# A gated recurrence beside a mixture of experts on one core: the recurrent products stream 2 columns in place of 20 or 40

## The chip, the cores and the metric

The kernel runs on one NeuronCore of a Trainium2 chip. The metric is device time in microseconds (us) of one execution. An execution with the profiler on was recorded as well; its instruction times are the source of every number below that is not a median.

## The reference, cut to what matters

The input `x` has shape (2, 1024, 256). A mixture of four experts plus a shared branch is added to it, and then a gated recurrence over the 1024 positions is added to that. The recurrence is serial in time:

```python
def step(h, xs):
    xzt, xrt, xht = xs
    z = jax.nn.sigmoid(xzt + h @ U_z + vz)
    r = jax.nn.sigmoid(xrt + h @ U_r + vr)
    hh = jnp.tanh(xht + r * h @ U + vh)
    h_new = (1.0 - z) * h + z * hh
    return (h_new, h_new)
...
x = x + _L0_cond_ref(x, cond_1024, ...)
x = x + _L1_cond_ref(cond_1024, x, ...)
```

The batch of `x` is B = 2, so the state has 2 rows of 256 numbers. With features on the 128 partitions, one recurrent product of one 128x128 weight tile has 2 columns of data.

## The kernel before, in words

The sequence is cut into 8 chunks of 128 positions, a chunk into 8 bodies of 16 steps: 64 bodies, 1024 steps. A chunk's hidden layer of 1024 is cut into 8 slices, so chunk c+1's feed-forward is 8 tiles, and one tile is done beside each body of chunk c. Chunk 0's feed-forward and the first tile of chunk 1 come before the recurrence starts.

All order on TensorE is written by hand. `gru_body` (L953) does a step as follows. It waits for the first half of the state (`h_parts`, HI), does the products of the reset gate R with it, three tiles of the update gate Z, then R's products with the low half of the state (LO), and the rest of Z. Then comes `gap_work` window 0. It waits for `p_parts` (reset gate times state, HI and LO, written by VectorE at L716 and L719), does the products of the candidate C, and then `gap_work` window 1. ScalarE takes the tanh of each gate (L507), VectorE makes the new state with scans at L730 and L732.

A recurrent product is made by `recur` (L911, its matmul is L918). Each gate has 4 weight tiles of 128x128; the weights are split in two fp16 parts, `u_high` and `u_mid`. HI is multiplied by both parts, LO by `u_high` alone, so a gate has 12 matmuls and a step 36. R and Z stream `H_FILL` = 20 columns, C streams `FILL` = 40. Only the first 2 carry data; the others are zeros, set once by VectorE in `p_parts` and `h_parts`, and are added to later columns of the same PSUM bank, to which they add nothing.

`gap_work` (L926) fills the time in which TensorE waits for the other engines. With a feed-forward tile it does units of it (`up` at L856, `down` at L874); a unit is half of one fp32 product of 256 columns, and the profile shows it as two matmuls of 128 columns. A tile has 40 units. The table `FFN_UNITS` gives window 0 one unit, window 1 one unit or, at t = 4 to 10, 12 and 14, two; at t = 15 the second window has none left. At t = 1 `turn_body` transposes the finished body. In the last body of a chunk, where a next chunk follows, `gate_input` (L888) is put into 12 windows, two matmuls of 256 columns each, and `output_bias` (L829) into t = 3. The last 8 bodies have neither; there `gap_work` issues idle matmuls on a constant tile (L950), one of 256 columns in window 0, two of 512 in window 1. Body 55 has `gate_input` but no feed-forward, and no idle matmuls.

`inject` (L903) starts a body by writing the input part of each gate into its PSUM bank, three matmuls of 64 columns a gate.

Of the kernel before, what the change touches and what calls it, by code (L numbers as in the profile page):

```python
# [27 lines left out]
F16 = mybir.dt.float16  # L28
# [3 lines left out]
P = 128  # L32
# [7 lines left out]

FILL = 40
H_FILL = 20
IDLE_FILL = (256, 512)


def moe_gru_kernel(nc, x, cond, gate_w, gate_b, time_w, time_b, ew1, eb1, ew2, eb2, sw1, sb1, sw2, sb2,
                   w_z, u_z, c_z, b_z, w_r, u_r, c_r, b_r, w_h, u_h, c_h, b_h, branch_mask, out):
    B, T, D = x.shape  # L50
    E, _, H = ew1.shape
    BR = E + 1
    KC = D // P
# [6 lines left out]
    SC = STEPS * B  # L60
    ST = KC * B
# [41 lines left out]
    with ctx:  # L103
        def sb(name, shape, dt=F32):
            return ctx.enter_context(nc.sbuf_tensor(name, shape, dt))

        def pb(name):
            return ctx.enter_context(nc.psum_tensor(name, [P, 512], F32))
# [56 lines left out]
        spread = sb("spread", [B, BR, B])  # L165


        p_parts = sb("p_parts", [P, 2, KC, FILL], F16)
        keep_warm = sb("keep_warm", [P, max(IDLE_FILL)], BF16)
        h_parts = sb("h_parts", [P, 2, FILL // B, 2 * ST], F16)  # L170
        HI, LO = range(2)
        blend = sb("blend", [P, 2 * ST])
        half_h = sb("half_h", [P, ST])
# [3 lines left out]
        gate_ps = [pb("r_ps"), pb("z_ps"), pb("c_ps")]  # L177
# [585 lines left out]
        def _(pe):  # L763
            mm = pe.matmul
# [5 lines left out]
            for i in range(CH):  # L770
# [7 lines left out]
                for k in range(KC):  # L778
                    for b in range(B):
                        at = (k * B + b) * P  # L780
                        last = pe.transpose(xp_ps[i % 2][:, at:at + P], x_rows[:, i, b, k * P:(k + 1) * P],
                                            ident[:, :])
# [27 lines left out]
            for g in range(GATES):  # L810
                for m in range(KC):
                    at = (g * KC + m) * B
                    for k in range(KC):
                        last = mm(gate_ps[0][:, at:at + B], cf[:, g, k, m * P:(m + 1) * P], cond_v[:, k, :],
                                  start=(g == 0 and m == 0 and k == 0), stop=(k == KC - 1),
                                  skip_group_check=True)
# [94 lines left out]
            def recur(g, t, part, i, weights, tile, stop=False):  # L911

                m, k = tile
                width = FILL if part is p_parts else H_FILL
                moving = (p_parts[:, i, k, :] if part is p_parts else
                          h_parts[:, i, 0:H_FILL // B, (2 * k) * B + 1:(2 * k + 2) * B:2])
                for at, w in enumerate(weights):
                    last = mm(gate_ps[g][:, m * SC + t * B:m * SC + t * B + width],  # L918
                              w[:, g, k, m * P:(m + 1) * P], moving, start=False,
                              stop=stop and k == KC - 1 and at == len(weights) - 1,  # L920
                              skip_group_check=True)
                return last
# [30 lines left out]
            def gru_body(n, ffn, tail, last):  # L953
                cols = chunk_columns(ffn[0]) if ffn else None
                tail_cols = chunk_columns(tail) if tail is not None else None
                for t in range(STEPS):
# [4 lines left out]
                    for tile in TILES:  # L961
                        recur(R, t, h_parts, HI, BOTH, tile)
# [3 lines left out]
                    for tile in TILES[:early]:  # L966
                        recur(Z, t, h_parts, HI, BOTH, tile)
                    pe.wait_ge(part_ready, before_n + 4)
                    for tile in TILES:
                        last_mm = recur(R, t, h_parts, LO, HIGH, tile, stop=True)  # L970
# [82 lines left out]
```

## Time and profile before

| | |
|---|---|
| median of 3 runs | 2317.78 us (2313.11 to 2319.58) |
| the profiled execution, its own time | 2310.71 us |
| its span | 2308.9 us |
| mean granted TensorE clock | 0.975 |
| TensorE busy (matmul) | 2157.9 us, 93% |
| VectorE, ScalarE, GpSimdE busy | 1200.4, 679.3, 344.0 us |

PE is TensorE's matmuls, PEld its weight loads, DVE VectorE, ACT ScalarE, POOL GpSimdE. A granted clock of 1.00 is TensorE's level of 2.4 GHz, 0.50 is that of 1.2 GHz. Matmuls overlap in the array: the time from one start to the next is what a product costs in a stream, the duration is how long one is in flight. A line with x4 merges four instructions that follow each other, from the first start to the last end.

### The profile page before, as it was taken

What the parts mean: (1) busy time and instruction counts of PE and PEld (TensorE: products, weight loads), DVE (VectorE), ACT (ScalarE), POOL (GpSimd) and SP (SyncE); (2) the same over time, 40 slices, a digit from 0 to 9 for tenths busy, and PEclk for the clock granted to TensorE, in tenths of its full rate; (3) what the DMA queues carried; (4) which work ended last, traced back from release to release, by engine and by line L of the source; (5) the groups of instructions that cost most, each with busy time, mean ns of one, the idle gap of its engine ahead of it and who ended that gap; (6) DMA issues with size and microseconds to landing.
All of it is one profiled execution on the core that took longest, in us unless ns stands there. A gap on an engine that the chain in (4) does not pass through costs nothing.

```text
span 2308.9 us, 108165 instructions
## 1 busy us (share of the span) xinstructions
PE 2157.9 (93%) x42955; PEld 1785.3 (77%) x43019; DVE 1200.4 (52%) x10473; ACT 679.3 (29%) x3670; POOL 344.0 (15%) x684
## 2 busy tenths in 40 slices
PE   7999999999999999999999999999999999988888
PEld 6787888887887888888888788888788888755555
DVE  5245555555545555555545555555554555555554
ACT  2332233232232232322233222323223223222222
POOL 3011111111111111111102111111111111110000
PEclk8999999999999999999999999999999999899999
DMA  5411111111111111111111111111111111000000
GB/s 159 125 55 45 44 41 40 44 41 43 45 38 45 43 42 41 45 40 45 41 40 45 40 47 39 40 45 40 45 43 40 40 45 42 11 4 4 4 4 4
DMA packets 143478, 97.21 MB, mean 42 GB/s; under 512 B 13664, under 2 KB 142999, under 8 KB 143004
## 3 DMA queue, kind: packets, MB, share of 16 engines
q1 hardware_dynamic: 141840, 90.49, 13.5%
q8 instruction: 338, 5.54, 1.0%
q14 instruction: 136, 1.11, 0.2%
q10 hardware_dynamic: 1164, 0.07, 0.0%
HBM read 88.41 MB, written 2.10 MB: 39 GB/s over the span
## 4 chain that ended last, share of the span: by engine, by line
PE 88%; DVE 5%; issue 4%; ACT 4%; POOL 0%; POOLq 0%; ACTq 0%; DVEq 0%
PE c_ps L918 22%; PE r_ps L918 19%; PE y_ps L874 15%; PE up_ps L856 13%; PE z_ps L918 12%; DVE h_parts L730 3%; ACT c_ps L507 2%; PE up_ps L950 2%; PE xp_ps L888 2%; DVE p_parts L716 1%; ACT r_ps L507 1%; PE xp_ps L898 1%; PE y_ps L829 0%; DVE hidden L278 0%; PE z_ps L903 0%
## 5 line engine op out<-in xcount | busy, mean ns | idle before, releaser
L918 PE MATMUL r_ps<-h_parts,u_high 128*128 128x20 f16 x8192 | 609.6, 180 | 82.3 <-DVE h_parts L730 49.9
L918 PEld LDWEIGHTS r_ps<-h_parts,u_high 128*128 128x128 f16 x8192 | 429.9, 96 | 260.3 <-DVE h_parts L730 149.5
L918 PEld LDWEIGHTS c_ps<-p_parts,u_high 128*128 128x128 f16 x8192 | 415.4, 96 | 203.1 <-DVE p_parts L716 139.1
L918 PE MATMUL c_ps<-p_parts,u_high 128*128 128x40 f16 x8192 | 530.8, 183 | 42.2 <-DVE p_parts L716 24.3
L918 PE MATMUL z_ps<-h_parts,u_high 128*128 128x20 f16 x8192 | 568.0, 179 | 0.0
L856 PE MATMUL up_ps<-feat,up_w 128*128 128x128 f32 (+1 forms) x2380 | 528.0, 315 | 0.0
L874 PE MATMUL y_ps<-hidden,down_w 128*128 128x128 f32 (+1 forms) x2380 | 507.9, 319 | 6.1 <-DVE hidden L278 6.1
L716 DVE SCALAR_TENSOR_TENSOR p_parts<-r_ps,h_hist 128x4 f16<-128x4 f32 x1024 | 165.9, 162 | 606.0 <-ACT r_ps L507 606.0
L918 PE MATMUL z_ps<-h_parts,u_mid 128*128 128x20 f16 x4096 | 439.6, 179 | 0.0
L918 PEld LDWEIGHTS z_ps<-h_parts,u_high 128*128 128x128 f16 x8192 | 427.8, 96 | 0.0
L507 ACT ACTIVATE r_ps<-r_ps 128x4 f32<-128x4 f32 x1024 | 161.8, 158 | 821.8 <-PE r_ps L918 821.8
L730 DVE TENSOR_TENSOR_SCAN h_parts<-c_ps,blend 128x8 f16<-128x8 f32 x1024 | 177.5, 173 | 387.7 <-ACT c_ps L507 387.7
L507 ACT ACTIVATE c_ps<-c_ps 128x4 f32<-128x4 f32 x1024 | 161.8, 158 | 711.9 <-PE c_ps L918 711.9
L874 PEld LDWEIGHTS y_ps<-hidden,down_w 128*128 128x128 f32 x2380 | 354.0, 197 | 16.3 <-issue 12.7
L856 PEld LDWEIGHTS up_ps<-feat,up_w 128*128 128x128 f32 x2380 | 358.2, 191 | 8.7 <-issue 3.0
L918 PE MATMUL c_ps<-p_parts,u_mid 128*128 128x40 f16 x4096 | 340.2, 180 | 0.0
L918 PE MATMUL r_ps<-h_parts,u_mid 128*128 128x20 f16 x4096 | 337.7, 179 | 0.0
L918 PEld LDWEIGHTS z_ps<-h_parts,u_mid 128*128 128x128 f16 x4096 | 299.0, 96 | 0.0
L918 PEld LDWEIGHTS c_ps<-p_parts,u_mid 128*128 128x128 f16 x4096 | 259.2, 97 | 4.9 <-issue 0.6
L918 PEld LDWEIGHTS r_ps<-h_parts,u_mid 128*128 128x128 f16 x4096 | 257.0, 97 | 6.9 <-issue 2.2
L722 DVE TENSOR_SCALAR blend<-z_ps,half_s 128x4 f32<-128x4 f32 x1024 | 218.6, 214 | 0.0
L719 DVE TENSOR_TENSOR p_parts<-r_ps,p_parts 128x4 f16<-128x4 f32 x1024 | 166.6, 163 | 35.6
(132 smaller groups left out, 2139.0 us busy)
## 6 DMA issues: line engine op xcount, KB each, us to landing
up_w<-in_L_cond_ew SPq DMA_DIRECT2D x256, 128.0 KB, 2.4
down_w<-in_L_cond_ew SPq DMA_DIRECT2D x256, 128.0 KB, 2.1
up_w<-in_L_cond_sw SPq DMA_DIRECT2D x64, 128.0 KB, 2.4
down_w<-in_L_cond_sw SPq DMA_DIRECT2D x64, 128.0 KB, 2.1
x_rows<-in_x SPq DMA_DIRECT2D x8, 256.0 KB, 5.0
out<-out_rows SPq DMA_DIRECT2D x128, 16.0 KB, 1.8
cf<-in_L_cond_C_r SPq DMA_DIRECT2D x1, 256.0 KB, 5.7
cf<-in_L_cond_C_z SPq DMA_DIRECT2D x1, 256.0 KB, 5.8
```

The costliest lines, as they stand in the source:

```text
L507: act.activation((c_now, tanh_r, tanh_z)[(g + 1) % GATES].rearrange("p (m b) -> p m b", b=B), gate_v[g][:, :, t, :], ACT.Tanh, scale=0.5 / ...
L716: dve.scalar_tensor_tensor(p(HI), tr, 1.0, prev, ALU.add, ALU.mult).then_inc(part_ready, 1)
L719: dve.tensor_tensor(p(LO), sq(product), p(HI), ALU.subtract).then_inc(part_ready, 1)
L722: dve.tensor_scalar(blend_v[:, :, 0], tz, 1.0, half_s[:, :], ALU.add, ALU.mult).then_inc(state, 1)
L730: dve.tensor_tensor_scan(h_parts[:, HI, 0, :], cand, blend[:, :], 0.0, ALU.mult, ALU.add).then_inc(part_ready, 1)
L856: last = mm(up_ps[e % 2][:, at:at + width], up_w[:, e, k, :], cols[k, half], start=(k == 0 and at == 0), stop=(k == KC - 1), skip_group_ch ...
L874: last = mm(y_ps[:, m * COLS + at:m * COLS + at + width], down_w[:, e, m * P:(m + 1) * P], hidden[:, e % 2, at:at + width], start=False, s ...
L888: last = mm(xp_ps[g % 2][:, m * COLS:(m + 1) * COLS], wx[:, g, k, m * P:(m + 1) * P], cols[k, None], start=(m == 0 and k == 0), stop=(k == ...
L898: last = pe.transpose(rows_ps[0:SC, k * P:(k + 1) * P], out_feat[:, k, :], ident[:, :])
L918: last = mm(gate_ps[g][:, m * SC + t * B:m * SC + t * B + width], w[:, g, k, m * P:(m + 1) * P], moving, start=False, stop=stop and k == K ...
L950: mm(up_ps[0][:, 0:IDLE_FILL[window]], ident16[:, :], keep_warm[:, 0:IDLE_FILL[window]], start=True, stop=True, skip_group_check=True)
```

## The change

Every recurrent product streams B = 2 columns. The two constants go, and the tiles shrink to the columns that carry data. The number and order of instructions, all waits, the idle matmuls and the feed-forward units stay.

```diff
-FILL = 40
-H_FILL = 20
 IDLE_FILL = (256, 512)
...
-        p_parts = sb("p_parts", [P, 2, KC, FILL], F16)
+        p_parts = sb("p_parts", [P, 2, KC, B], F16)
         keep_warm = sb("keep_warm", [P, max(IDLE_FILL)], BF16)
-        h_parts = sb("h_parts", [P, 2, FILL // B, 2 * ST], F16)
+        h_parts = sb("h_parts", [P, 2, 1, 2 * ST], F16)
...
             def recur(g, t, part, i, weights, tile, stop=False):

                 m, k = tile
-                width = FILL if part is p_parts else H_FILL
                 moving = (p_parts[:, i, k, :] if part is p_parts else
-                          h_parts[:, i, 0:H_FILL // B, (2 * k) * B + 1:(2 * k + 2) * B:2])
+                          h_parts[:, i, 0, (2 * k) * B + 1:(2 * k + 2) * B:2])
                 for at, w in enumerate(weights):
-                    last = mm(gate_ps[g][:, m * SC + t * B:m * SC + t * B + width],
+                    last = mm(gate_ps[g][:, m * SC + t * B:m * SC + t * B + B],
                               w[:, g, k, m * P:(m + 1) * P], moving, start=False,
                               stop=stop and k == KC - 1 and at == len(weights) - 1,
                               skip_group_check=True)
```

## Rows read from the trace of the kernel before

**Rows 1.** The page: busy time of TensorE, and its granted clock in 40 slices.
```profile
PE 2157.9 (93%) x42955; PEld 1785.3 (77%) x43019; DVE 1200.4 (52%) x10473; ACT 679.3 (29%) x3670; POOL 344.0 (15%) x684
...
PEclk8999999999999999999999999999999999899999
```

**Rows 2.** The page: shares of the chain that ended last, by engine.
```profile
PE 88%; DVE 5%; issue 4%; ACT 4%; POOL 0%; POOLq 0%; ACTq 0%; DVEq 0%
```

**Rows 3.** Groups by line and form; busy us, mean ns of one, then idle time before.
```profile
L918 PE MATMUL c_ps<-p_parts,u_high 128*128 128x40 f16 x8192 | 530.8, 183 | 42.2 <-DVE p_parts L716 24.3
```

**Rows 4.** Timeline of a one-unit step at full clock: start us, us, instruction.
```profile
1032.35 0.18 PE L918 MATMUL r_ps<-h_parts,u_high 128*128 128x20 f16 x1
...
1032.72 0.25 PE L918 MATMUL r_ps<-h_parts,u_high 128*128 128x20 f16 x4
...
1033.01 0.16 ACT L507 ACTIVATE r_ps<-r_ps 128x4 f32<-128x4 f32 x1 [0.92 <-PE r_ps L918]
...
1033.42 0.19 PE L918 MATMUL c_ps<-p_parts,u_high 128*128 128x40 f16 x1
...
1033.69 0.27 PE L918 MATMUL c_ps<-p_parts,u_high 128*128 128x40 f16 x4
...
1033.99 0.16 ACT L507 ACTIVATE c_ps<-c_ps 128x4 f32<-128x4 f32 x1 [0.68 <-PE c_ps L918]
1034.42 0.18 PE L918 MATMUL r_ps<-h_parts,u_high 128*128 128x20 f16 x1
```

**Rows 5.** Busy time by stretch, all engines; after POOL the granted clock, DMA share, GB/s.
```profile
123.00:2043.00 1920.00, 1819.25 (x37572) 1547.30 (x37572) 1012.22 (x9064) 579.41 (x3164) 305.81 (x616) 0.97 0.14 41
...
401.00:404.40 3.40, 3.02 (x71) 2.49 (x70) 1.73 (x17) 1.08 (x5) 0.61 (x1) 1.00 0.12 36
404.50:407.90 3.40, 3.40 (x54) 3.32 (x51) 1.67 (x15) 1.15 (x6) 0.73 (x1) 0.50 0.02 5
...
2029.30:2032.60 3.30, 2.11 (x59) 1.67 (x54) 1.72 (x15) 1.06 (x7) 0.00 (x0) 1.00 0.01 2
2032.70:2042.80 10.10, 8.17 (x170) 6.24 (x172) 5.01 (x46) 2.49 (x15) 4.58 (x11) 0.50 0.01 2
```

**Rows 6.** The same view, PE records of L856 (`up`) alone, with the clock.
```profile
401.10:404.50 3.40, 1.37 (x6) 1.00 0.10 30
...
414.70:418.10 3.40, 0.78 (x5) 1.00 0.13 38
```

**Rows 7.** The same stretches, PE records of L874 (`down`) alone.
```profile
401.10:404.50 3.40, 0.06 (x1) 1.00 0.10 30
...
414.70:418.10 3.40, 1.16 (x6) 1.00 0.13 38
```

**Rows 8.** Timeline of a two-unit step at half clock: start us, us, instruction.
```profile
1911.24 0.23 PE L918 MATMUL r_ps<-h_parts,u_high 128*128 128x20 f16 x1
...
1911.66 0.26 PE L918 MATMUL r_ps<-h_parts,u_high 128*128 128x20 f16 x4
...
1911.93 0.77 PE L874 MATMUL y_ps<-hidden,down_w 128*128 128x128 f32 x2
1911.96 0.16 ACT L507 ACTIVATE r_ps<-r_ps 128x4 f32<-128x4 f32 x1 [0.96 <-PE r_ps L918]
...
1912.50 0.24 PE L918 MATMUL c_ps<-p_parts,u_high 128*128 128x40 f16 x1
...
1912.80 0.30 PE L918 MATMUL c_ps<-p_parts,u_high 128*128 128x40 f16 x4
1912.94 1.20 PE L856 MATMUL up_ps<-feat,up_w 128*128 128x128 f32 x4
...
1913.93 0.23 PE L918 MATMUL r_ps<-h_parts,u_high 128*128 128x20 f16 x1
```

**Rows 9.** Timeline at half clock: two idle matmuls of window 1.
```profile
2041.64 1.06 PE L950 MATMUL up_ps<-keep_warm,ident 128*128 128x512 bf16 x2
```

**Rows 10.** Timeline of ScalarE: the first tanh of the recurrence.
```profile
123.85 0.16 ACT L507 ACTIVATE r_ps<-r_ps 128x4 f32<-128x4 f32 x1 [1.80 <-PE r_ps L918]
```

## The prediction

> **What bounds the kernel now.** I read the page first. TensorE is busy 93% of the span and its granted clock is nearly full in every slice [rows 1]; the chain of waits gives it 88% of the path [rows 2]. A share says little here, because TensorE runs filler and feed-forward work in its gaps, so I went to the timeline. The recurrence starts at about 123 us [rows 10], and all 1024 steps come after it. In the step of [rows 4] TensorE is not the limit. R's first product starts at 1032.35 and the next step's at 1034.42, 2.07 us later. Between them lies one serial chain: R's products, tanh at 1033.01, VectorE, C's first product at 1033.42, C's products, tanh at 1033.99, the scan, and the next R at 1034.42. From the tanh of R to C's first product is 0.41 us, from the tanh of C to the next R 0.43 us. The feed-forward lies beside this chain as long as it fits into those gaps. The widths to be cut: 40 columns for C, 183 ns a product in flight [rows 3], 20 for R [rows 4] and alike for Z.
>
> **The change, part by part, at full clock.** The instruction count stays, so the price of a product is its spacing and the latency of the last one. Spacing: the x4 line of R lasts 0.25 us, one of them 0.18, so three spacings are 0.07 and one is 25 ns (rounded) [rows 4]. The x4 line of C cannot be used for this, because its wait for the low half widens it. But 12 products of C at 40 columns, 17 ns of streaming at 2.4 GHz, cannot be below those 25 ns, and 20 columns are 8 ns. [...] Saving: nothing. Latency: R's last product starts at 1032.72 + 0.07 = 1032.79, its tanh at 1033.01, 0.22 later. C's last starts at 1033.69 + 0.09 = 1033.78, its tanh at 1033.99, 0.21 later [rows 4]. Twenty columns and forty have the same delay, although 20 columns are 8 ns of streaming. So at full clock I take zero for the whole edit. Bounds: a loss has no source in fewer columns at an equal clock; a gain is at most the streaming itself, 18 columns of R and 38 of C, 7.5 + 16 = 23.5 ns, 24 us over 1024 steps. The shorter memsets lie before 123 us behind the feed-forward and the waits for matrices, and are nothing.
>
> [...]
>
> **The change, the clock.** This is the step I weigh most. The clock is at half in some pieces of the recurrence, 0.97 on average from 123 to 2043 us [rows 5]. What did TensorE do before it fell? From 2029.3 to 2032.6, still at full clock, it had only recurrent products (59 records, no idle matmul, no feed-forward); from 2032.7 on it was at half [rows 5]. From 401.1 to 404.5 it had the light steps at the start of a body, 6 + 1 feed-forward records [rows 6, 7], and fell at 404.5 [rows 5]; from 414.7 to 418.1, in heavier steps, it had 5 + 6 such records and stayed at full [rows 6, 7]. It was not idle before the fall at 404.5, but busy 3.02 of 3.40 us [rows 5]. It fell where the least arithmetic was streamed, and recurrent products alone, filler and all, did not hold it.
>
> Now count a step in column passes. A feed-forward record at 1.2 GHz has 213 ns: four records fill 1912.94 to 1913.93 [rows 8], 0.99 us less 0.14 of turn-over (what two records take there above 2 x 213, 1911.93 to 1912.50), which is 256 cycles for 128 columns, two passes. A light step (two units, four records) has 4 x 256 = 1024 passes and 24 x 20 + 12 x 40 = 960 of the recurrence, 1984 in all, and after such steps the clock has fallen. After the change the heaviest ordinary step (three units) has 1536 + 36 x 2 = 1608, the light one 1096. So every ordinary step will stream less than those after which the clock fell. The zeros seem to do nothing but carry the clock. I forecast the half clock through nearly the whole recurrence.
>
> **Price of a step at half clock, 2 columns.** From [rows 8]: R and Z take 1911.24 to 1911.93, 0.69 us; the x4 line is 0.26, a spacing of 27 ns, so 20 columns (17 ns at 1.2 GHz) are hidden here too, and 0.69 stays. One unit: 1911.93 to 1912.50, 0.57. C's block: 1912.50 to 1912.94, 0.44, at (0.30 - 0.20)/3 = 33 ns a product, which is 40 columns at 1.2 GHz; at 2 columns it goes down to the 27 of R, 11 x 6.7 = 0.07 less, 0.37. Two units: 0.99. A two-unit step is 0.69 + 0.57 + 0.37 + 0.99 = 2.62 us and TensorE has no gap in it. In a one-unit step the second half is 0.37 + 0.57 = 0.94 by TensorE, but by the chain 0.34 to the start of C's last product, 0.21 to its tanh and 0.43 to the next R, 0.98; the step is 1.26 + 0.98 = 2.24. (R's tanh at 1911.96 comes 0.22 after the last R product, as at full clock.)
>
> **The sum.** A body has 7 one-unit steps (t = 15 counted so) and 9 two-unit steps: 15.7 + 23.6 = 39.3 us, plus some 0.6 for six injections of 64 columns at 53 ns and the transposes, an estimate: 39.9. Of 55 bodies with feed-forward, 49 are ordinary: 1955. Six end a chunk and add 24 `gate_input` records of 256 columns, 427 ns each, and four of `output_bias`: 12 us, 51.9 each; these stream most, the clock may come back inside them, so I take 50: 300. Body 55 has no feed-forward: 16 x 2.1 and about 6 for `gate_input`: 40. In the last 8 bodies a step is 0.72 (R to its tanh [rows 8]) + 0.41 + C's 0.34 + the two idle matmuls of 512 columns, 427 ns each at 1.2 GHz (1.06 together with the latency of the last [rows 9]), 0.85, 2.33 us; 16 steps and 0.4 are 37.7, times 8 is 302. With 123 before and 5 behind: 123 + 1955 + 300 + 40 + 302 + 5 = 2725 us. That is against the profiled execution, span 2308.9 and time 2310.71, 2 us apart; the median of the runs is 7 above it. I predict 2730. What late work is next? VectorE, ScalarE and the transfers keep their times, so with slower TensorE they only wait longer; nothing new comes onto the path.
>
> **Rivals.** (A) Half clock nearly throughout: 2730. (B) It alternates: in the heavier steps the clock comes back. For: pieces at half end by themselves, and those steps keep their feed-forward. Against: they stream less per time than the steps at half clock in [rows 8], which carried 960 passes more. If seven of nine two-unit steps return to 2.07, 49 x 7 x 0.55 = 189 us go, and 37 in the last 8 bodies with them at full clock (33.1 a body): about 2510. (C) The clock cares for work in flight, not for columns: TensorE keeps issuing a product every 25 ns, nothing changes, 2318, or a few us more with more pieces at half. Against it is the fall at 404.5 us, with TensorE busy before it [rows 5]. [...] (D) The other side: the clock holds and latency falls with the columns. Its place is the last product of R and of C, its price the 23.5 ns a step, its condition that the delay of 0.21 to 0.22 is not a floor: 2294. (That the change doesn't do what it says is excluded: both branches of `moving` and the output go to 2 columns.)
>
> **How the numbers follow.** A 0.75, B 0.13, C 0.07, D 0.05. The bound for no change is 0.3%, 7 us, about what this measurement can tell. C falls half or so inside it: same 0.06, faster 0.05, slower 0.89. A alone holds 2640 (clock back in the last 8 bodies and in the chunk ends) to 2770 (transitions and waits that the sum leaves out). To leave out no more than 2 in 10 the range goes on to B's middle: 2530 to 2770.
>
> **What would show it.** In the changed profile the PEclk line should stand at 5 from about the fourth slice to the end; the mean clock about 0.55. C's spacing at half clock should be 27 ns, not 33; a two-unit step 2.62 us, a one-unit step 2.24; the delay to the tanh 0.22 for all gates. TensorE's idle time before C should vanish in feed-forward steps. I am wrong if the line keeps 9 over most slices (C or D), or shows 7 to 8 (B); if steps at half clock cost other than 2.24 and 2.62, the sum is.

## The result, and the profile after

| | before | after |
|---|---|---|
| median of 3 runs | 2317.78 us | 2679.53 us (2667.41 to 2679.92) |
| profiled execution, time and span | 2310.71, 2308.9 us | 2679.92, 2678.1 us |
| mean granted clock | 0.975 | 0.537 |
| matmul records in the trace | 42955 (64 missing; weight loads 43019) | 43019 |

The change makes the kernel slower, by a ratio of 1.156 (95% interval 1.1504 to 1.1616). The forecast was 2730, within 2530 to 2770. The work is the same; TensorE does nearly all of the recurrence at a granted clock of 0.50.

The page of the changed kernel, the lines that answer to [rows 1, 2], and two groups by line (answering to [rows 3]; the recurrent matmuls are on L915 now, the tanh on L505, the feed-forward on L854 and L872, the idle matmuls on L947):

```profile
PE 2626.8 (98%) x43019; PEld 2351.0 (88%) x43019; DVE 1198.8 (45%) x10473; ACT 686.9 (26%) x3670; POOL 344.9 (13%) x684
...
PEclk8955556555565555555565555655556555555555
...
PE 95%; DVE 2%; ACT 2%; issue 1%; DMA 0%; SPq 0%; POOL 0%; POOLq 0%; ACTq 0%; DVEq 0%
...
L915 PE MATMUL r_ps<-h_parts,u_high 128*128 128x2 f16 x8192 | 618.9, 169 | 20.5 <-DVE h_parts L728 19.6
...
L915 PE MATMUL c_ps<-p_parts,u_high 128*128 128x2 f16 x8192 | 519.7, 170 | 9.4 <-DVE p_parts L714 2.6
```

The clock line stands at 5 from the third slice on, with a 6 in five slices. TensorE's share rises from 93% to 98% and its share of the chain from 88% to 95%. Its idle time before C's products falls from 42.2 to 9.4 us. In the nine two-unit steps of a body it is the bound throughout: R's first product starts 0.63 us after the start of the scan that makes the state (L728), where it was 0.23. In most one-unit steps (t = 0, 2, 11, 15) that stays 0.23 us, so there the second half of the step still goes by the chain. VectorE's busy time is that of before to 2 us. A product is in flight for less time than before, 170 ns against 183, and yet everything takes longer. The busy times by stretch, in the columns of [rows 5]:

```profile
130.00:415.00 285.00, 283.08 (x4775) 267.24 (x4775) 128.75 (x1155) 72.10 (x393) 38.05 (x75) 0.50 0.12 35
417.00:433.00 16.00, 15.81 (x293) 13.93 (x291) 7.23 (x65) 6.50 (x31) 1.34 (x2) 1.00 0.18 51
434.00:744.00 310.00, 307.79 (x5140) 289.40 (x5138) 138.67 (x1244) 78.89 (x428) 42.60 (x86) 0.50 0.13 36
...
2360.00:2670.00 310.00, 300.58 (x5206) 187.87 (x5204) 147.84 (x1328) 65.93 (x408) 22.28 (x56) 0.50 0.01 3
```

The clock falls as soon as the recurrence begins, at 126.5 us. It comes back for 14 to 17 us in each of the six bodies that have feed-forward and `gate_input` together, and falls again. From 2048 us on it never comes back, in body 55 (`gate_input` without feed-forward) as little as in the last 8. TensorE is busy 99% of the first of these stretches: the clock is low with the engine supplied. Now single steps, to set beside [rows 8, 9]:

```profile
1011.14 0.24 PE L915 MATMUL r_ps<-h_parts,u_high 128*128 128x2 f16 x4
...
1011.40 0.77 PE L872 MATMUL y_ps<-hidden,down_w 128*128 128x128 f32 x2
1011.42 0.16 ACT L505 ACTIVATE r_ps<-r_ps 128x4 f32<-128x4 f32 x1 [1.01 <-PE r_ps L915]
...
1012.23 0.24 PE L915 MATMUL c_ps<-p_parts,u_high 128*128 128x2 f16 x4
1012.34 1.20 PE L872 MATMUL y_ps<-hidden,down_w 128*128 128x128 f32 x4
1012.51 0.16 ACT L505 ACTIVATE c_ps<-c_ps 128x4 f32<-128x4 f32 x1 [0.78 <-PE c_ps L915]
...
1013.75 0.24 PE L915 MATMUL r_ps<-h_parts,u_high 128*128 128x2 f16 x4
...
2500.40 0.21 PE L915 MATMUL r_ps<-h_parts,u_high 128*128 128x2 f16 x1
...
2502.72 0.21 PE L915 MATMUL r_ps<-h_parts,u_high 128*128 128x2 f16 x1
```

A two-unit step lasts 13.75 - 11.14 = 2.61 us, a step of the last bodies 2.32. C's x4 line is 0.24 where it was 0.30 at this clock. And from the last product (1011.14 + 0.08) to the tanh at 1011.42 there are 0.20 us, for C (1012.23 + 0.08 to 1012.51) as well: less than the 0.21 to 0.22 of [rows 4].

The prediction's 2.4 and 1.2 GHz stand for columns a ns. In the kernel before, two idle matmuls of 512 columns in a row last 0.59 us at a clock of 1.00 and one alone 0.38 (2103.95 and 2102.10 us), so they start 0.21 us apart: 2.4 columns a ns. At 0.50 the two last 1.06 [rows 9], each 0.63, and start 0.43 us apart: 1.2 columns a ns.

### The profile page after: what moved, and what is told of

It is laid out like the page before. It is cut to its first block, busy times and chain, and to the rows that moved or that the text cites. A ratio compares the mean times of both kernels' runs of the same rounds, so it can differ in the third digit from the quotient of the medians.

```text
span 2678.1 us, 108229 instructions
## 1 busy us (share of the span) xinstructions
PE 2626.8 (98%) x43019; PEld 2351.0 (88%) x43019; DVE 1198.8 (45%) x10473; ACT 686.9 (26%) x3670; POOL 344.9 (13%) x684
## 4 chain that ended last, share of the span: by engine, by line
PE 95%; DVE 2%; ACT 2%; issue 1%; DMA 0%; SPq 0%; POOL 0%; POOLq 0%; ACTq 0%; DVEq 0%
PE up_ps L854 25%; PE y_ps L872 25%; PE c_ps L915 13%; PE r_ps L915 12%; PE z_ps L915 11%; PE up_ps L947 4%; PE xp_ps L886 2%; PE xp_ps L896 1%; DVE p_parts L714 1%; ACT r_ps L505 1%; PE y_ps L827 1%; DVE h_parts L728 1%; ACT c_ps L505 0%; PE z_ps L901 0%; PE c_ps L901 0%
## 5 line engine op out<-in xcount | busy, mean ns | idle before, releaser
L854 PE MATMUL up_ps<-feat,up_w 128*128 128x128 f32 (+1 forms) x2380 | 829.2, 463 | 0.0
L872 PE MATMUL y_ps<-hidden,down_w 128*128 128x128 f32 (+1 forms) x2380 | 782.0, 457 | 5.4 <-DVE hidden L276 5.4
L915 PE MATMUL r_ps<-h_parts,u_high 128*128 128x2 f16 x8192 | 618.9, 169 | 20.5 <-DVE h_parts L728 19.6
L915 PEld LDWEIGHTS r_ps<-h_parts,u_high 128*128 128x128 f16 x8192 | 516.0, 107 | 129.9 <-DVE h_parts L728 87.8
L854 PEld LDWEIGHTS up_ps<-feat,up_w 128*128 128x128 f32 x2380 | 575.0, 302 | 13.3 <-issue 4.9
L915 PE MATMUL z_ps<-h_parts,u_high 128*128 128x2 f16 x8192 | 579.2, 165 | 0.0
L872 PEld LDWEIGHTS y_ps<-hidden,down_w 128*128 128x128 f32 x2380 | 557.0, 303 | 15.9 <-issue 12.3
L915 PE MATMUL c_ps<-p_parts,u_high 128*128 128x2 f16 x8192 | 519.7, 170 | 9.4 <-DVE p_parts L714 2.6
L915 PEld LDWEIGHTS c_ps<-p_parts,u_high 128*128 128x128 f16 x8192 | 462.1, 105 | 52.6 <-DVE p_parts L714 45.0
L915 PEld LDWEIGHTS z_ps<-h_parts,u_high 128*128 128x128 f16 x8192 | 459.3, 104 | 0.0
L915 PE MATMUL z_ps<-h_parts,u_mid 128*128 128x2 f16 x4096 | 441.4, 165 | 0.0
L505 ACT ACTIVATE r_ps<-r_ps 128x4 f32<-128x4 f32 x1024 | 161.8, 158 | 1078.1 <-PE r_ps L915 1078.1
L728 DVE TENSOR_TENSOR_SCAN h_parts<-c_ps,blend 128x8 f16<-128x8 f32 x1024 | 177.6, 173 | 499.0 <-ACT c_ps L505 499.0
L505 ACT ACTIVATE c_ps<-c_ps 128x4 f32<-128x4 f32 x1024 | 161.8, 158 | 814.0 <-PE c_ps L915 814.0
L915 PEld LDWEIGHTS r_ps<-h_parts,u_mid 128*128 128x128 f16 x4096 | 303.5, 112 | 53.8 <-issue 8.7
L915 PEld LDWEIGHTS c_ps<-p_parts,u_mid 128*128 128x128 f16 x4096 | 311.2, 114 | 34.4 <-issue 5.9
L915 PE MATMUL r_ps<-h_parts,u_mid 128*128 128x2 f16 x4096 | 333.6, 165 | 0.0
L915 PE MATMUL c_ps<-p_parts,u_mid 128*128 128x2 f16 x4096 | 333.1, 165 | 0.0
L915 PEld LDWEIGHTS z_ps<-h_parts,u_mid 128*128 128x128 f16 x4096 | 323.1, 104 | 0.0
```

The source lines that it names most:

```text
L505: act.activation((c_now, tanh_r, tanh_z)[(g + 1) % GATES].rearrange("p (m b) -> p m b", b=B), gate_v[g][:, :, t, :], ACT.Tanh, scale=0.5 / ...
L728: dve.tensor_tensor_scan(h_parts[:, HI, 0, :], cand, blend[:, :], 0.0, ALU.mult, ALU.add).then_inc(part_ready, 1)
L854: last = mm(up_ps[e % 2][:, at:at + width], up_w[:, e, k, :], cols[k, half], start=(k == 0 and at == 0), stop=(k == KC - 1), skip_group_ch ...
L872: last = mm(y_ps[:, m * COLS + at:m * COLS + at + width], down_w[:, e, m * P:(m + 1) * P], hidden[:, e % 2, at:at + width], start=False, s ...
L915: last = mm(gate_ps[g][:, m * SC + t * B:m * SC + t * B + B], w[:, g, k, m * P:(m + 1) * P], moving, start=False, stop=stop and k == KC - ...
```

## The experiments

The open questions were whether streamed columns, and not something else in the edit, carry the clock; whether they must be in the recurrent products; and what width costs in itself. Every kernel below is timed against the kernel before on the same chip. Its median there lay between 2314 and 2321 us.

**1. Wider products of the state** (from the kernel before).

```diff
-H_FILL = 20
+H_FILL = 40
```

> R and Z stream 40 columns in place of 20, C 40 as before. [...] Rival (columns cost 1/2.4 GHz each, as C's 40 seem to): 40 stay hidden, and with more columns the pieces at half clock vanish: 2295 us.

Measured: 2551.17 us, ratio 1.1014 (1.0983 to 1.1046), clock 0.988. Slower at a full clock. My estimate, 2480 us with 33 ns between two of the state's products, was too low, and the rival's 2295 us has fallen. Timeline of this kernel:

```profile
1002.75 0.20 PE L918 MATMUL r_ps<-h_parts,u_high 128*128 128x40 f16 x1 [0.23 <-DVE h_parts L730]
...
1002.97 0.21 PE L918 MATMUL r_ps<-h_parts,u_high 128*128 128x40 f16 x1
...
1025.37 0.25 PE L918 MATMUL c_ps<-p_parts,u_high 128*128 128x40 f16 x4
```

The first two lines are the first and the last of seven products: six spacings in 0.22 us are 37 ns. The last line is C: its 40 columns, which lie side by side in memory, fit into 25. The state's columns are read in pairs, two elements apart, each pair 8 elements after the one before it. At half clock the state's 40 take no less: from 2217.80 us on, at 0.50, twelve spacings of this kernel take 0.46 us, 38 ns each, where C's 40 are 33 apart. So the 20 of R and the 40 of C of [rows 4] are hardly a narrow and a wide product: from these numbers I estimate 37/2 = 18.5 ns at full clock for 20 columns read that way, and 40/2.4 = 17 for the 40 of C.

**2. The last product of R and of C alone narrow** (from the kernel before).

```diff
                 width = FILL if part is p_parts else H_FILL
+                if i == LO and g != Z and tile == TILES[-1]:
+                    width = B
-                moving = (p_parts[:, i, k, :] if part is p_parts else
-                          h_parts[:, i, 0:H_FILL // B, (2 * k) * B + 1:(2 * k + 2) * B:2])
+                moving = (p_parts[:, i, k, 0:width] if part is p_parts else
+                          h_parts[:, i, 0:width // B, (2 * k) * B + 1:(2 * k + 2) * B:2])
```

> All widths as before except the very last product of R and of C in a step, which streams 2 columns; 56 columns a step go. Theory (the delay from the last product to the tanh falls with its columns: 200 ns in the changed kernel against 216 before): 16 ns less twice a step where the chain decides, 20 to 33 us, 2285 to 2298 us. Rival (a floor of 216 ns at full clock, as the prediction took it; the 200 came from elsewhere): 2318 us or a little more, from more pieces at half clock.

Measured: 2297.64 us, ratio 0.9922 (0.9889 to 0.9955), clock 0.963. Two products of 36 are narrow (a merged line shows the form of its first product), and the step goes from 2.07 to 2.03 us:

```profile
1001.43 0.24 PE L920 MATMUL r_ps<-h_parts,u_high 128*128 128x20 f16 x4
...
1001.71 0.16 ACT L507 ACTIVATE r_ps<-r_ps 128x4 f32<-128x4 f32 x1 [0.90 <-PE r_ps L920]
...
1003.46 0.24 PE L920 MATMUL r_ps<-h_parts,u_high 128*128 128x20 f16 x4
```

Two steps' x4 lines are 2.03 us apart. To the ns the usual step goes from 2.067 to 2.033, which times 1024 is some 35 us; 22 arrive (2319.2 to 2297.64). The mean clock is lower, 0.963 in the median run where the kernel before had 0.970 beside it, and I put the rest there; that is argued, not shown. The delay from the last product to the tanh is 0.201 us for R and C, where it was 0.216: it does fall with the columns of the last product, at full clock too.

**3, 4. Half of the zeros** (from the kernel before; the state's tile keeps its size). The third kernel has `H_FILL = 2`, the fourth `FILL = 2`.

> C keeps 40 columns, R and Z stream 2: 528 columns a step where before had 960 and the change 72. Theory (columns of any product carry the clock): a state between, light steps at half clock, the clock back in part of the heavy steps: 2450 to 2620 us, and within 1.5% of the kernel that keeps the 20 of R and Z alone (504 columns). Rival (the zeros of the state products or those of C matter by their place): one of the two is at 2318 and the other at 2680.

> R and Z keep 20 columns, C streams 2: 504 columns a step. Theory: as for the kernel that keeps C's 40 alone, 2450 to 2620 us. Rival: all of one side, 2318 or 2680 us.

Measured: 2731.15 us, ratio 1.1788 (1.1755 to 1.1821), clock 0.553, and 2666.47 us, ratio 1.1495 (1.1463 to 1.1528), clock 0.547. Both expectations failed: half the zeros give next to none of the time back (the change itself has a ratio of 1.156). The clock is at half whichever half it is. The third kernel by stretch, 130 to 1990 us:

```profile
130.00:1990.00 1860.00, 1844.12 (x30318) 1729.85 (x30318) 814.35 (x7302) 472.22 (x2549) 248.61 (x497) 0.53 0.12 35
```

The fourth:

```profile
130.00:1990.00 1860.00, 1844.54 (x31289) 1734.54 (x31287) 840.71 (x7536) 486.84 (x2629) 256.64 (x514) 0.53 0.13 36
```

The third is even slower than the change, because C's 40 columns are 33 ns apart at half clock and not 27 [rows 8].

**5. The columns moved into idle matmuls beside the feed-forward** (from the changed kernel).

```diff
+                if ffn and tail is None:
+                    mm(xp_ps[0][:, 0:IDLE_FILL[window]], ident16[:, :], keep_warm[:, 0:IDLE_FILL[window]],
+                       start=True, stop=True, skip_group_check=True)
```

> The changed kernel (2 columns everywhere), with one idle matmul of 256 columns in window 0 and one of 512 in window 1 of each step that has feed-forward and no gate_input; they write a PSUM bank that nothing reads then. 768 columns of ones stand for the 888 of zeros that went. Theory (the clock asks for streamed columns, wherever they come from): full clock through most of the recurrence, step 2.05 us where the gaps hold them and up to 0.2 more where they are full, 2380 to 2500 us, mean clock over 0.9. Rival (the columns must be in the recurrent products, or it was never the columns): the clock stays at half and the idle matmuls cost 0.64 us a step, 3000 us or more.

Measured: 3142.33 us, ratio 1.3551 (1.3496 to 1.3606), clock 0.534. The rival's number. Time by stretch at the beginning of the recurrence:

```profile
130.00:137.00 7.00, 7.00 (x155) 5.54 (x153) 3.89 (x35) 1.99 (x11) 1.96 (x4) 1.00 0.10 28
137.80:145.00 7.20, 7.20 (x95) 6.28 (x96) 2.59 (x24) 1.77 (x9) 0.73 (x1) 0.50 0.13 39
```

It fell in the first body's light steps, at 137.8 us, and never had a stretch at full clock again outside of the bodies that end a chunk. Either idle columns do not count, or they were too few there and nothing brings the clock back. The later kernels tell these apart.

**6. Narrow products in the last 8 bodies alone** (from the kernel before; `narrow[0]` is set by `gru_body`).

```diff
-                width = FILL if part is p_parts else H_FILL
+                width = B if narrow[0] else FILL if part is p_parts else H_FILL
...
+                narrow[0] = n >= CH * BODIES - BODIES
```

> As before, but 2 columns in the last 8 bodies, those with idle matmuls and no feed-forward. Theory: the idle matmuls alone do not hold the clock there; these 128 steps go to half clock at 2.32 us each where they had 2.07, 33 us more, 2350 us. Rival (the last stretch keeps its clock on the idle matmuls, 1280 columns a step, and the change lost its time only beside the feed-forward): 4 us less than before, 2314 us.

Measured: 2349.87 us, ratio 1.0149 (1.0115 to 1.0182), clock 0.915. Without the zeros the clock stays at half, although each step still has 1280 idle columns:

```profile
2043.00:2090.00 47.00, 46.02 (x795) 28.41 (x792) 22.39 (x202) 10.05 (x62) 2.75 (x7) 0.50 0.01 4
...
2110.00:2290.00 180.00, 176.29 (x3037) 109.36 (x3034) 85.38 (x765) 37.68 (x235) 13.70 (x35) 0.50 0.01 3
```

It had fallen before these bodies, in body 55, at 2030.1 us. So this kernel shows that the idle columns do not bring the clock back; whether they alone would hold a full clock it does not ask. In the kernel before, the clock falls in body 55 as well and is back by 2043 us:

```profile
2043.00:2090.00 47.00, 41.84 (x885) 27.13 (x893) 25.37 (x228) 11.29 (x71) 2.75 (x7) 1.00 0.02 4
```

**7, 8. Wider still.** From the kernel before with `FILL = 56` and `H_FILL = 28`; the seventh has the narrow last products of the second as well.

> C streams 56 columns, R and Z 28, which a spacing of 25 ns should just hide, and the last product of R and of C streams 2. Theory: steps of 2.033 us as with the last product narrow at the old widths, and the pieces at half clock that stand in the kernel before go: 2270 to 2280 us, clock over 0.98. Rival (the widths are no longer hidden): spacing over 25 ns, steps of 2.07 or more, 2310 us or more.

> The same widths of 56 and 28 without the narrow last products. Theory: 7 ns more of delay before each tanh, steps of 2.08 us, and no pieces at half clock: 2305 to 2325 us; the difference to the kernel with narrow last products is 40 to 48 us. Rival (the pieces at half clock hardly cost anything and width costs nothing): 2318 us and no more than 35 us of difference.

Measured: 2294.16 us, ratio 0.99 (0.9868 to 0.9932), clock 0.987, and 2328.08 us, ratio 1.0057 (1.0038 to 1.0077), clock 0.986. The clock is better than before in both and the step is longer than hoped, mostly 2.05 to 2.07 us in the seventh and 2.09 to 2.11 in the eighth, where before has 2.07. Both lie above their forecasts, the seventh by 14 us. The eighth, with every product wide, loses to the kernel before although its clock is higher. Width is paid for in the delay to the tanh (0.223 to 0.225 us for 0.216) and in the spacing (C's is mostly 26 ns for 25). The 34 us between the two are what the two narrow products are worth; 40 to 48 were expected, and no more than 35 by the rival.

**9. Many more idle columns in the last 8 bodies** (from the sixth kernel).

```diff
-                    for _ in range(1 + window):
-                        mm(up_ps[0][:, 0:IDLE_FILL[window]], ident16[:, :], keep_warm[:, 0:IDLE_FILL[window]],
+                    for wide in ((512, 512), (512, 512, 256))[window]:
+                        mm(up_ps[0][:, 0:wide], ident16[:, :], keep_warm[:, 0:wide],
```

> As before, but in the last 8 bodies the recurrent products stream 2 columns and the idle matmuls are two of 512 in window 0 and 512, 512 and 256 in window 1: 2304 idle columns and 72 of the recurrence a step, where before had 1280 and 960. They fit in the gaps at full clock. Theory (streamed columns hold the clock, in whichever product): full clock in the last 8 bodies, steps of 2.03 to 2.06 us, 2310 us. Rival (the zeros have to ride in the recurrent products, or idle matmuls don't count): half clock from 2030 us on, and 2304 columns take 1.92 us a step, so steps of 3 us: 2430 us.

Measured: 2431.05 us, ratio 1.0483 (1.045 to 1.0516), clock 0.895. Again the rival's number. But the clock was at half already when these bodies began, from 2037.7 us on, since body 55 has no idle matmuls (in the kernel before, too, it is at half from 2032.7 us [rows 5], and comes back at 2043). Whether idle columns can hold a full clock was thus not asked.

**10. The same beside the feed-forward, with more columns** (from the kernel before). The products are narrow in the 49 ordinary bodies with feed-forward, and idle matmuls bring each of their steps to 2376 passes.

```diff
+                narrow[0] = ffn is not None and tail is None
...
+                if ffn and tail is None:
+                    units = len(FFN_UNITS[t, window])
+                    for wide in (512,) if window == 0 else {0: (512, 512, 256), 1: (512, 256), 2: (256,)}[units]:
+                        mm(xp_ps[0][:, 0:wide], ident16[:, :], keep_warm[:, 0:wide],
+                           start=True, stop=True, skip_group_check=True)
```

> As before, but in the 49 bodies with feed-forward and without gate_input the recurrent products stream 2 columns, and idle matmuls make up every step to 2376 passes (a feed-forward record of 128 columns counted as 256): 512 columns in window 0, 768 in window 1 beside one unit, 256 beside two, 1280 beside none. The kernel with 768 idle columns in every step had 1864 in the light steps, fell there and never came back; before had 1984 to 2496. Theory (columns, and the light steps decide because a step at half clock is too long to bring it back): full clock nearly throughout, 0.95 or more, steps of 2.05 to 2.15 us, 2310 to 2400 us. Rival (idle matmuls don't carry the clock beside feed-forward): half clock, 3000 us or more.

Measured: 2635.27 us median of 6 runs, from 2439.45 to 2708.56, too scattered for a ratio. The profile (span 2565.3 us, clock 0.842) shows why:

```profile
135.00:360.00 225.00, 224.75 (x4776) 195.87 (x4776) 121.85 (x1092) 67.15 (x372) 35.40 (x71) 1.00 0.16 44
372.00:637.00 265.00, 263.72 (x5552) 229.23 (x5551) 141.88 (x1269) 81.26 (x443) 43.27 (x87) 1.00 0.15 43
...
670.00:1035.00 365.00, 365.00 (x4926) 298.47 (x4924) 124.55 (x1117) 70.04 (x382) 37.65 (x75) 0.50 0.10 28
1050.00:1310.00 260.00, 258.97 (x5471) 225.53 (x5469) 138.99 (x1245) 79.89 (x437) 42.65 (x86) 1.00 0.15 44
1350.00:1715.00 365.00, 365.00 (x4920) 298.48 (x4917) 124.67 (x1119) 69.95 (x381) 37.20 (x74) 0.50 0.10 28
```

The same code holds the full clock for whole chunks, then sits at half for the ordinary bodies of a whole chunk, then at full again. A chunk's seven ordinary bodies take 233 us at full clock (396 to 629 us) and 367 at half (667.6 to 1034.9). Those 134 us are also about the distance between the times of the six runs: 2439, twice 2567, and three from 2703 to 2709. The profiled run, of 2567 us, has two such chunks at half; that the others have one and three is an estimate from these numbers.

The changed kernel, with the same narrow products, lost the clock at 126.5 us, at once. This one begins at full clock as well and holds it through the first chunk. TensorE is busy all the time in both. Idle columns do carry the clock, so one of the two readings of the fifth kernel falls. What they do not do is bring it back.

**11. The ninth kernel, begun with the clock at full.** The edit is that of the ninth, from body 58 on; bodies 56 and 57 are as before.

> The kernel with narrow products and 2304 idle columns at the end, once more, but from body 58 on, not 56: bodies 56 and 57 are as before, so that the clock is back at full when the narrow products begin. Theory (idle columns hold a clock that is full, as beside feed-forward, but do not bring back one that is at half, because at half the step grows with them): full clock from 2050 us to the end, steps of 2.03 to 2.06 us, 2315 us. Rival (in this stretch, without feed-forward, idle columns do not carry the clock at all): it falls soon after body 58 starts, steps of 2.88 us, 2390 us.

Measured: 2312.47 us, ratio 0.9996 (0.9978 to 1.0014), clock 0.975. The theory's number: the clock holds, with steps of 2.03 us, and the time is that of the kernel before. The ninth kernel in a stretch of its last bodies:

```profile
2110.00:2290.00 180.00, 180.00 (x2562) 106.00 (x2561) 68.60 (x616) 29.76 (x186) 11.27 (x28) 0.50 0.01 3
```

This kernel in the same stretch:

```profile
2110.00:2290.00 180.00, 175.62 (x3600) 116.71 (x3658) 98.41 (x885) 42.75 (x270) 12.12 (x31) 1.00 0.02 4
```

Identical instructions in each body there, 2562 of them in 180 us or 3600, by the clock at which the stretch was entered.

**12. The version that beats both.** From the kernel before, with the narrow last products of the second and

```diff
-FILL = 40
-H_FILL = 20
+FILL = 48
+H_FILL = 24
```

> C streams 48 columns, R and Z 24, and the last product of R and of C streams 2. Theory: 48 columns at full clock are 20 ns, well inside a spacing of 25, so the steps are 2.033 us (56 and 28 gave 2.05), with fewer pieces at half clock than with 40 and 20: 2278 to 2290 us, the fastest so far. Rival (the spacing grows with any width over 40): steps of 2.05, 2295 us.

Measured: 2281.49 us, ratio 0.9833 (0.9802 to 0.9863), clock 0.989: the fastest kernel of the study. Steps are 2.04 us, between the theory's 2.033 and the rival's 2.05, so the eight columns more are nearly hidden. In the recurrence beside the feed-forward, the second kernel (40 and 20) and then this one:

```profile
130.00:1990.00 1860.00, 1777.77 (x36716) 1532.72 (x36711) 986.30 (x8843) 572.02 (x3086) 299.44 (x598) 0.97 0.15 42
130.00:1990.00 1860.00, 1771.02 (x37083) 1511.87 (x37079) 1000.84 (x8948) 577.77 (x3121) 298.73 (x600) 0.99 0.15 42
```

It gets 8948 VectorE instructions done in these 1860 us, at a clock of 0.99, where the second kernel gets 8843, at 0.97.

## Why the prediction was right, and where it was off

**The clock: right.** It named the half clock through nearly the whole recurrence, and that is what came: 0.537 on average, and 0.50 in every long stretch. Its ground, that a step of the changed kernel streams less than steps after which the clock had fallen before, was a comparison of columns. It is now shown by kernels that put other columns in their place and hold the clock (10 and 11), and by 3 and 4, where neither half of the zeros was enough. Rival C, by which work in flight is what counts, has fallen: TensorE is busy for 283.08 of 285 us at half clock.

**The price of a step at half clock: right.** Two-unit steps 2.62 forecast, 2.61 measured; steps in the last bodies 2.33 and 2.32; C's block with the spacing of R. This came out because the trace before had short pieces at half clock, in which every term could be read.

**The sum: 47 us too high**, span 2678.1 against 2725. By the first tanh of each body, an ordinary body takes 39.52 us where the sum had 39.9, 49 x 0.38 = 18 us less. Most of it is the 0.6 us of injections and transposes, an estimate: the steps that have them (t = 0 and 1) take 2.43 us, 0.4 together above 2.24. The other one-unit steps are 2.19 to 2.26 for 2.24. The delay to the tanh, taken as 0.21 to 0.22 and now 0.20 us, can matter in these alone, since TensorE is the bound in the two-unit steps. The six bodies at the chunk ends take 271 us together for 300. The clock does come back inside them, as the prediction said it might, for about 14 us each, and I had taken off 2 us a body, and they lie nearly 7 below the 51.9 of the sum.

**"At full clock I take zero for the whole edit": wrong.** The step of the prediction that failed is "Twenty columns and forty have the same delay, although 20 columns are 8 ns of streaming". The delays are the same, 0.216 us, but neither is a floor: at full clock the third kernel has 0.201 for R's 2 columns and 0.217 for C's 40, the fourth 0.216 for R's 20 and 0.201 for C's 2. By the estimate above R's strided 20 weigh about as much as C's 40. Going to 2 saves 34 ns a step at full clock (2.07 to 2.03 us, kernel 2), more than the 23.5 ns that stood as the outer bound. The streaming that this bound is made of fits C, 16 ns and 15 measured, and is half of what R's strided columns show, 7.5 against 15. So rival D's mechanism exists and is worth 35 us over the recurrence; it lost because its condition, a clock that holds, did not. The change gained some 15 ns of delay only where the chain still decides, and lost about 0.55 us in each two-unit step. The spacing was taken right: with 2 columns too it is 25 ns at full clock (changed kernel, six spacings from 2040.72 to 2040.87 us); what sets it is not shown.

**Rival B** did not occur in the ordinary bodies: once at half, the clock stays there, 290 to 311 us at a time, into the last body of the chunk. I had counted columns per step only. At half clock a feed-forward step is longer too, so the same columns are spread over 2.61 us in place of 2.07, and what little would hold a full clock does not restore it. That reading fits 9 against 11 and the two faces of 10, where a step of 2376 passes takes 2.06 us or 3.25. It is the state's persistence that those kernels show; that the spread of the columns is its cause is argued, not shown.

## What to carry to other kernels

Columns of zeros cost nearly nothing here while they fit under the spacing that a product has anyway (25 ns; 48 and 24 columns are in the fastest kernel, 2281.49 us), and here they kept TensorE's clock up (0.975 with them, 0.537 without). Look at the granted clock before taking "useless" work out, and price every step at both levels from short pieces at half clock in the trace. Put that filler into the many products that nobody waits for, and leave narrow the last one before a semaphore, whose width is paid for as delay (0.216 us with 20 or 40 columns, 0.201 with 2). Filler in idle matmuls held a full clock here but did not win it back (9, 10, 11), so such a stretch must be entered at full clock.

## What the runs showed that was not expected

- With filler in idle matmuls the kernel has two lasting states: whole chunks at full or at half, 2439 to 2709 us for one program. In the profiled run the clock was lost both times within about 1 us of a chunk's first body (668.5 and 1347.7 us), after it had been full through most of the body before.
- The state's columns, read in pairs two elements apart, cost more than C's: products with 40 of them are 37 ns apart at full clock and 38 at half, C's 40 are 25 apart and 33. At half clock 20 of them still fit under 27 ns [rows 8].
- Half the filler is worth next to nothing: 528 or 504 columns a step of 960 gave 2731 and 2666 us, against 2680 with 72.
